# A tile's last transposes four steps later, and a block's last look-up copied straight from its bank

## What is computed

```python
e = jnp.stack([tbl_0[ids[:, 0]], ..., tbl_25[ids[:, 25]]], axis=1)      # 2048 x 26 x 128
combined = jnp.concatenate([dense[:, None, :], e], axis=1)              # 2048 x 27 x 128
inter = jnp.einsum('bfd,bgd->bfg', combined, combined)[:, IU0, IU1]     # 351 pairs
h = jnp.concatenate([dense, inter, dense], axis=1)                      # 607
h = jnp.maximum(h @ W_top1 + b_top1, 0.0)                               # 512
h = jnp.maximum(h @ W_top2 + b_top2, 0.0)                               # 256
y = h @ W_top3
```

## Time and profile before

| | |
|---|---|
| time, median of 3 runs | 380.4 us (379.95 to 380.72) |
| profiled execution, its own time | 379.88 us |
| its span, first to last instruction | 378.1 us |
| mean granted TensorE clock | 0.985 of full speed |
| busy: PE | 336.4 us (89%) |
| busy: POOL | 269.8 us (71%) |
| busy: DVE | 243.6 us (64%) |
| busy: ACT | 193.1 us (51%) |

### The profile page before, as it was taken

One profiled execution on the slowest core, in us unless ns is written; L12 is line 12 of the kernel. 1 busy time (PEld: TensorE's weight loads), 2 busy tenths in 40 slices (PEclk: granted clock), 3 DMA queues, 4 the chain that ended last, 5 costly groups with the idle time before them and its releaser, 6 DMA issues.

```text
span 378.1 us, 8112 instructions
## 1 busy us (share of the span) xinstructions
PE 336.4 (89%) x3360; PEld 275.0 (73%) x3360; DVE 243.6 (64%) x174; ACT 193.1 (51%) x261; POOL 269.8 (71%) x276
## 2 busy tenths in 40 slices
PE   0989888989896899899999999898989969899887
PEld 0757667877774687788876788787876758668776
DVE  3979998889999759777887269697770030302132
ACT  2899985273755281746344473536345463543200
POOL 6777787777787777777777777777777777776020
PEclk9999999999998999999999999999999989998999
DMA  7997944699976357884537367852437322634210
GB/s 196 266 267 200 275 114 124 163 275 267 234 192 176 91 144 217 216 207 123 160 77 227 83 177 196 222 155 59 105 76 223 84 56 56 185 82 113 77 22 3
DMA packets 37540, 58.46 MB, mean 155 GB/s; under 512 B 20635, under 2 KB 21621, under 8 KB 37504
## 3 DMA queue, kind: packets, MB, share of 16 engines
q1 hardware_dynamic: 28296, 40.62, 39.7%
q0 software_dynamic: 8512, 16.95, 17.9%
q10 hardware_dynamic: 696, 0.38, 0.3%
HBM read 47.68 MB, written 10.23 MB: 153 GB/s over the span
## 4 chain that ended last, share of the span: by engine, by line
PE 32%; POOL 28%; issue 12%; DVE 8%; DMA 7%; SPq 6%; ACT 6%; ACTq 0%; DVEq 0%
POOL rows L713 28%; PE look_bank L773 13%; DVE one_hot L1078 6%; SPq L650 5%; PE out_bank L814 4%; PE short_bank L869 4%; PE out_bank L819 4%; DMA whole_table<-in_tbl 3%; PE out_bank L803 3%; PE short_bank L854 2%; DMA rows<-in_tbl,all_ids 2%; ACT one_hot L911 2%; ACT one_hot L918 2%; ACT high_table L900 1%; SPq L639 1%
## 5 line engine op out<-in xcount | busy, mean ns | idle before, releaser
L713 POOL DMA_INDIRECT rows<-in_tbl,all_ids x256 | 262.8, 1027 | 79.3 <-issue 75.6
L1078 DVE TENSOR_TENSOR one_hot<-spread_ids,row_bank 128x2048 fp32r<-128x2048 int32 (+3 forms) x80 | 170.9, 2173 | 20.1 <-PE look_bank L773 16.4
L773 PE MATMUL look_bank<-one_hot,high_table 125*128 125x512 f32 x328 | 137.8, 420 | 14.1 <-DVE low_table L1066 10.9
L773 PE MATMUL look_bank<-one_hot,low_table 125*128 125x512 f32 x328 | 130.5, 398 | 0.0
L773 PEld LDWEIGHTS look_bank<-one_hot,high_table 125*128 125x128 f32 x328 | 63.1, 192 | 33.1 <-DVE low_table L1066 10.0
L773 PEld LDWEIGHTS look_bank<-one_hot,low_table 125*128 125x128 f32 x328 | 63.3, 193 | 15.5 <-issue 2.9
L869 PEld LDWEIGHTS short_bank<-all_combined 128*59 128x59 f32 x2048 | 57.8, 134 | 13.2 <-issue 13.0
L869 PE MATMUL short_bank<-all_combined 128*59 128x54 f32 x2048 | 60.6, 219 | 5.5 <-ACT all_combined L945 2.9
L1091 DVE COPY all_combined<-short_bank 128x512 f32<-128x512 f32 x32 | 21.5, 688 | 68.2 <-PE short_bank L854 67.7
L926 ACT COPY looked_up<-look_bank 128x512 f32<-128x512 f32 x40 | 23.3, 585 | 71.4 <-PE look_bank L773 71.1
L973 ACT COPY all_dots<-short_bank 128x432 f32<-128x432 f32 x64 | 32.7, 520 | 30.7 <-PE short_bank L869 27.2
(11 more groups left out here) (44 smaller groups left out, 189.1 us busy)
## 6 DMA issues: line engine op xcount, KB each, us to landing
whole_table<-in_tbl SPq DMA_DIRECT2D x26, 448.0 KB
spread_ids<-in_ids_by_feature SPq DMA_DIRECT2D x40, 256.0 KB, 4.5
block_scratch<-all_dots SPq DMA_DIRECT2D x24, 208.0 KB
rows<-in_tbl,all_ids POOLq DMA_INDIRECT x256
block_scratch<-all_dots SPq DMA_DIRECT2D x24, 104.0 KB
pairs<-block_scratch SPq DMA_DIRECT2D x72, 29.2 KB
whole_table<-in_tbl SPq DMA_DIRECT2D x26, 52.0 KB
whole_table<-in_tbl SPq DMA_DIRECT2D x2, 560.0 KB
```

The costliest lines, as they stand in the source:

```text
L713: nc.gpsimd.indirect_dma_start(rows[:, t % ROW_TILES, slot, :], None, tables[SLOT_FEATURES[slot]][:, :], bass.IndirectOffsetOnAxis(ap=all_ ...
L773: last = nc.tensor.matmul(look_bank[s % LOOK_BANKS][:], table_parts[part][TABLE_PLACE[s]][0:ROWS_K, c, :], one_hot[0:ROWS_K, (chunks_befor ...
L1078: last = nc.vector.tensor_tensor(one_hot[:, place:place + n, :], spread_ids[:, s % ID_PLACES:s % ID_PLACES + 1, :].to_broadcast([P, n, COLS]),
```

## The change

A constant `LAST_TURN_AFTER = 4` and a branch in `steps_after`: for every tile but the last two, the next tile's fourth turn stands behind the first four steps of `work_after(t)` and no longer right behind the third turn. ACT's copy of this group moves along, since `copy_ends` follows the list; and `turned_done`, which GpSimd waits for, reaches a tile's full count four steps later. Tile 0's turns, and those of tile 15, stay where they were.

For the first tile of each block the last two looks are no longer moved together: the last but one is moved when its own look has been copied, and the last is copied by a new `move_last_look` from its bank's first 128 columns straight into `combined`, ahead of the copy of the whole bank to `looked_up`, which the other three tiles need.

```diff
--- before.py
+++ after.py
@@ -101,6 +101,8 @@
 
 OUTS_AFTER = [4, 6, 7, 7]
 
+LAST_TURN_AFTER = 4
+
 FIRST_MOVES = [8, 8, 8, 8]
 
 HALF_AHEAD = 12
@@ -286,6 +288,9 @@
     if t == TILES - 2:
 
         ahead = ahead[:-1] + out_steps(LAST - 1)[-1:] + out_steps(LAST)[:HALF_AHEAD] + ahead[-1:]
+    elif t + 1 < TILES:
+        work = work_after(t)
+        return ahead[:-1] + work[:LAST_TURN_AFTER] + ahead[-1:] + work[LAST_TURN_AFTER:]
     return ahead + work_after(t)
 
 
@@ -324,7 +329,8 @@
 def move_parts(t):
 
     m, u = divmod(t, PER_BLOCK)
-    return [(0, FIRST_MOVES[m]), (FIRST_MOVES[m], IN_BLOCK[m])] if u == 0 else [(0, IN_BLOCK[m])]
+    n = IN_BLOCK[m]
+    return [(0, FIRST_MOVES[m]), (FIRST_MOVES[m], n - 1), (n - 1, n)] if u == 0 else [(0, n)]
 
 
 def out_number(v, i):
@@ -946,6 +952,14 @@
                                    looked_up[:, place:place + b - a, u * P:(u + 1) * P].rearrange("d n p -> d p n")).then_inc(
                                        look_moved, 1)
 
+            def move_last_look(s):
+
+                m = BLOCK_OF[s]
+                act.wait_ge(half_done, 2 * (s + 1))
+                wait_for_tile(m * PER_BLOCK)
+                nc.scalar.copy(combined[:, :, 1 + GATHERED[m] + LOOK_SLOT[s]], look_bank[s % LOOK_BANKS][:, 0:P]).then_inc(
+                    look_moved, 1)
+
             def copy_dense(t):
                 m, u = divmod(t, PER_BLOCK)
                 v, place = unit_of(t)
@@ -1010,14 +1024,16 @@
                             copy_group(t, g)
                     elif kind == "look":
                         s, = of
+                        m = BLOCK_OF[s]
+                        if s == FIRST_LOOK[m + 1] - 1:
+                            move_last_look(s)
                         copy_look(s)
-                        m = BLOCK_OF[s]
                         for ahead in high_after(s):
                             high_part(ahead)
                         if s == FIRST_MOVES[0] - 1:
                             move_looks(0, 0, FIRST_MOVES[0])
-                        if s == FIRST_LOOK[m + 1] - 1:
-                            move_looks(m * PER_BLOCK, FIRST_MOVES[m], IN_BLOCK[m])
+                        if s == FIRST_LOOK[m + 1] - 2:
+                            move_looks(m * PER_BLOCK, FIRST_MOVES[m], IN_BLOCK[m] - 1)
                         if s + SPLIT_AHEAD in ACT_HOTS[1:]:
                             make_half(2 * (s + SPLIT_AHEAD) + 1)
                     elif of[0] < LAST:
```

## The result

The changed kernel takes 377.4 us in the median (22 executions) against 379.95 (22): a ratio of 0.9921, 95% interval 0.9900 to 0.9942, so 3.0 us (2.2 to 3.8) faster. The forecast was 381.3, slower. Single executions of either kernel lie some 1.5 us around their median, so a profile is one draw. The profiled execution of the changed kernel took 376.77 us, span 375.0.

The account below looks back on a forecast made before the run. GpSimd's gather queue was taken to bound the kernel. To 380.4 us came +0.3 for tile 3's later gather, +0.6 for the clock and 0 for collisions: 381.3 us, range 378.6 to 383.3.

Parts of the forecast that it names:

- What bounds the kernel: Whole kernel: GpSimd's queue of 256 gathers runs without a wait, 341 us; PE follows it, and the end hangs on it.
- (1): Last group's transposes behind four steps: some 13 us of PE waits removed, none credited; tile 3's gather could be held.
- (2): Last look's own copy at block ends: products 0.7 us sooner; leaves tile 3's gather +0.3 us late (0 to +1.1).
- (3): Tile 15's third group: PE's wait for rows grows to 3.35 us, the clock may fall sooner: +0.6 us (0 to +1.1).
- (4): Gathers held by DVE subtractions, 21 us in all: costs drawn anew, no change in the mean, spread 1.6 us.
- lucky collisions: Rival, chance 0.13: in GpSimd's queue the 28 subtractions fall better by at least 1.7 us; 379.6 or less, typically 379.
- MEET: Experiments' theory: PE's work and GpSimd's queue end about equally late, so shortening one alone gains less than it saves.

Follow-up runs that it names:

- e15: Kernel before, with the three subtractions for looks 15 to 17 reading PSUM (their low parts left out): ratio 0.9933, 2.5 us faster.
- e17: Changed kernel with two GpSimd memsets as pauses, ahead of the gathers of tiles 6 and 7: 0.9983 of the kernel before, 1.9 us slower than e18.
- e5: Kernel before, with the low-part subtractions taking their second input from PSUM (low part wrong): ratio 0.9874, 4.8 us faster.
- e18: The changed kernel itself, measured once more on the same chip as e17: 0.9933 of the kernel before.
- e13: Kernel before plus the last look's own copy, with turns moved only behind the products of tiles 8 to 13: ratio 1.0021, no gain.
- e2: Kernel before plus only the last look's own copy, no turn moved: ratio 1.0027, no gain.
- e19: Changed kernel with tile 15's third turn behind the third layer's step and six products, second measurement: 0.9892 of the kernel before, 4.1 us faster.
- e1: Kernel before plus only the moved turns, without the last look's own copy: ratio 0.9977, 0.9 us faster.
- e20: Same kernel as e19, but tile 1's fourth turn stays right behind its third: 0.9857 of the kernel before, 5.4 us faster.
- e6: Changed kernel with the low-part subtractions reading PSUM as in e5: 0.9791 of the kernel before, from four executions.
- e16: e13 with the three subtractions for looks 15 to 17 reading PSUM as in e15: 0.9910 of the kernel before, 3.4 us faster.

## Why the prediction was wrong, step by step

- **What bounds the kernel**: right in the main. e15 and e17 move the end by about what they move in GpSimd's queue. One limit was missing: in e5 the queue's end came 11 us sooner and the kernel's only 4.8; and in e18 PE waits for ACT and not for rows at tile 15.
- **(1), waits removed, nothing credited**: right. Some 13 us were to go; 5.5 net went (8.5 for copies and ACT gone, 3.0 for rows added). e13, with the late waits removed, and e2 gain nothing.
- **(1) and (2), tile 3's release**: the mechanism was right, and the size in one profile too: 0.17 us (forecast 0.3), 0.93 without the own copy (forecast up to 1.1). But e18 and e19 show 1.44 and 1.43 with the own copy, above the bound: in e18 GpSimd was there 0.69 us sooner (67.87 instead of 68.56) and tile 1's group ended 0.59 later (69.34 instead of 68.75). From that group's end to the gather it took 0.27 us in both (forecast 0.1 to 0.3). The own copy took 0.41 us (forecast 0.4), and the wait ahead of the products is 0.71 shorter (forecast 0.7).
- **(3), the clock**: the mechanism is in e1, where the wait at tile 15 grew to 2.54 us and the clock was 0.50 behind it; the size was too small there, since the stretch from that group to the products took 12.17 us, 1.6 more than before, with a bound of 1.1. In the changed kernel's first profile the longer wait and the fall came at tile 14 instead, ahead of tile 15's rows, and the tail kept its clock; in e18's it did not (11.03 us). The prediction asked for a wait of some 3 us for rows there and said it is wrong if that doesn't grow: in neither profile did it. Whether +0.6 holds in the mean is not settled.
- **(4), the collisions**: this is the step that failed. "These costs are drawn anew: no change in the mean" holds for a shift of unknown size. Here the first two subtractions cost 0.47 to 0.60 and 0.53 to 0.54 us in all six profiles of an unchanged front, and 0 to 0.01 and 0.40 to 0.43 in all ten with moved early turns: a shift, and no draw. The third is drawn anew (0 to 1.04), but from 1.04, the most that any gather had lost, so it could only fall. Whether the trace of before would have given the shift (2.3 to 3.8 us) closely enough was not tried. The term was 0 with a spread of 1.6; it measured -2.2 us over all gathers (the six kernels against the ten) and -2.6 for the five subtractions in the profiled pair (3.82 to 1.20). In that pair the other gathers took 1.3 back, so the prediction's own sign, a mean gather shorter by more than 0.01 us, was not met there (1.027 to 1.022); in e18 it was (1.007). The rule cited there from the Trainium skill (SBUF — State Buffer, "Who interferes with whom"), that the two exclude each other, agrees where both start together: with starts 0.01 us apart (87.92 and 87.93) the gather kept its 0.94 us and the subtraction took 1.27, with 0.06 between them the gather took 1.98 and the subtraction 1.23. A gather that is under way for 0.05 us or more leaves the subtraction at its usual time (1.21 to 1.23 us, 1.48 to 1.49 for the two larger ones).
- **The rivals**: what happened is the one called *lucky collisions*, at 0.13; it asked for at least 1.7 us. Most of it is no luck, as it comes again in profile after profile; the third subtraction's part of it, 0.5 us in the mean, is drawn.

The account of the 3.0 us: the gathers' 2.2 less 0.55 for the larger gaps at tile 3 (mean of nine kernels, e20 left out, 0.85 instead of 0.30) gives 1.65; the last gather starts at 342.32 in the mean of the six and at 340.93 in that of the eight without pauses or e20, 1.4 sooner. That is about half. What brings the other 1.6 us (0.8 to 2.4 by the interval of the ratio) is open. It should lie behind the last gather, but the traces don't show it there: with tile 15's third turn in its old place, the time of the profiled execution less the start of its last gather is 36.9 us in the mean of five of the six and 36.6 in that of six of the eight, with single profiles from 35.0 to 38.5. A part by MEET, in which PE's shorter way counts once the queue is shorter, is not excluded: e6 and e16 leave room for it. That the last two subtractions count is argued from the table: no run frees these two alone.

## What to carry to other kernels

Where one engine's queue runs without a wait, price an edit first by what it does to that queue; the waits that it took from another engine alone gained nothing here (e2, e13). Before calling collisions random, list each with its two starts, shift both by the edit's own numbers, and see which fall elsewhere (nobody has tried here how well that forecasts): a subtraction that began 0.06 us ahead of a gather cost 1.04 us, one 0.01 us ahead nothing, and three freed gathers showed at the end, 250 us later. Do not name a cause from one pair of profiles when single executions scatter by half the effect: the fall of the clock at the end caught the eye here, and the turn nearest to it moved nothing by itself.

## What the runs showed of the hardware that was not expected

- Collisions repeat: the costs of the first three subtractions agree within 0.13 us each in six profiles of different kernels, 90 to 106 us into the run, and that at 272 to 275 us is 0.79 or 0.80 in five of the six kernels whose late turns stay.
- A collision's cost follows from the two starts. In the 18 profiles other than e5's and e6's, 418 gathers start 0.044 to 1.05 us behind the start of a subtraction with both inputs in SBUF, and each ends 0.78 to 0.86 us behind the subtraction's end. Those that start 0.043 us behind or sooner keep their 0.94 us.
- Two executions of one program need not agree elsewhere: the changed kernel's mean gather was 1022 ns with a gap of 0.47 at tile 3 in one profile and 1007 with 1.74 in another, spans 375.0 and 375.4.
- With one input in PSUM the same subtraction holds no gather: 965 ns a gather against 1027.
- In the first pair of profiles a granted clock of 0.50 cost 1.6 to 1.7 us on 24 or 16 products (5.30 or 6.87 to 6.90 or 8.56). In e1, e16 and e17, with 2.35 to 3.02 us of wait for rows ahead of tile 15's third group, the stretch from that group to the products took 12.17 to 12.19 us instead of 8.8, 3.3 more.
